# Edge sums of a graph layer: a plain addition with a source slot from a table, and index registers loaded in blocks

## What is computed

```
e     = edge_attr @ We                       # per edge
kj    = k[src] + e
alpha = sum(q[dst] * kj, per head) / sqrt(32)
ea    = exp(alpha - max over the edges of the same dst)
msg   = (v[src] + e) * ea
out   = segment_sum(msg, dst) / segment_sum(ea, dst) + x @ Ws + bs
```

## Time and profile before

| | |
|---|---|
| median of three runs | 2568.09 us |
| span of the profiled execution (the page gives no other time of it) | 2568.6 us |
| first and last rescale of the edge loop (start) | 284.0 and 1957.4 us |
| TensorE busy | 2382.9 us, 93% of the span |
| VectorE busy | 2037.0 us, 79% |
| GpSimd busy | 1811.8 us, 71% |
| ScalarE busy | 1577.5 us, 61% |

### The profile page before, as it was taken

The page is one execution under the profiler, slowest core; times in us unless marked ns, Lnnn a source line. Parts: engine busy times, 40 slices in busy tenths (PEclk is TensorE's granted clock), DMA queues, the critical chain, the costliest instruction groups (busy, mean ns, idle before and its releaser), DMA issues. The chain is left out here.

```text
span 2568.6 us, 67072 instructions
## 1 busy us (share of the span) xinstructions
PE 2382.9 (93%) x13310; PEld 1992.2 (78%) x13311; DVE 2037.0 (79%) x5261; ACT 1577.5 (61%) x4373; POOL 1811.8 (71%) x2136
## 2 busy tenths in 40 slices
PE   6998999999999999999999999999995657999998
PEld 2445788888888888888888888888883646999998
DVE  6865899999999999999999999999997773222222
ACT  1222677777777677777767777767774224666665
POOL 4123788888888888888888888888886104666666
PEclk9999999999999999999999999999998557999999
DMA  7326777777777777777777777777772753433443
GB/s 229 128 107 187 231 227 221 227 228 228 223 227 227 220 230 224 221 227 226 227 221 226 227 225 229 227 218 220 228 223 78 227 162 60 71 63 64 70 66 55
DMA packets 337693, 476.68 MB, mean 186 GB/s; under 512 B 61318, under 2 KB 268492, under 8 KB 337052
## 3 DMA queue, kind: packets, MB, share of 16 engines
q0 software_dynamic: 92576, 259.72, 37.8%
q1 hardware_dynamic: 238492, 213.23, 28.0%
q10 hardware_dynamic: 6288, 0.05, 0.1%
HBM read 425.40 MB, written 50.57 MB: 185 GB/s over the span
## 5 line engine op out<-in xcount | busy, mean ns | idle before, releaser
L809 POOL DMA_INDIRECT kv_ring<-vk_table,tab_c x880 | 860.6, 978 | 284.3 <-issue 208.2
L963 PE MATMUL ps_e<-we_sb,aT 128*128 128x256 f32 x3520 | 919.5, 384 | 27.9 <-DVE ve_ke L1050 21.6
L963 PEld LDWEIGHTS ps_e<-we_sb,aT 128*128 128x128 f32 x3520 | 601.0, 191 | 102.8 <-issue 48.6
L1044 DVE TENSOR_TENSOR ve_ke<-kv_ring,ps_e 128x512 f32<-128x512 f32 x880 | 599.9, 682 | 38.1 <-PE ps_e L967 24.0
L1014 PE MATMUL ps_u<-ve_ke,sel 128*128 128x264 f32 x1760 | 547.7, 393 | 20.3 <-DVE node_slots L1114 6.8
L819 POOL TENSOR_TENSOR ve_ke<-ve_ke 128x256 f32<-128x256 f32 x880 | 553.4, 633 | 18.5 <-ACT factor L936 4.9
L967 PE MATMUL ps_e<-q_slots,selT 128*128 x1760 | 517.6, 375 | 0.0
L896 ACT COPY aT<-ps_t 128x256 f32<-128x256 f32 x880 | 325.5, 370 | 310.1 <-PE ps_t L951 189.6
L1114 DVE SCALAR_TENSOR_TENSOR node_slots<-node_slots,same_tile,ps_u 128x264 f32 x880 | 423.0, 481 | 29.5 <-DVE node_slots L1099 10.6
L967 PEld LDWEIGHTS ps_e<-q_slots,selT 128*128 128x128 f32 x1760 | 335.1, 190 | 45.9
L1032 DVE TENSOR_REDUCE alpha<-ve_ke 128x8 f32<-128x256 f32 x880 | 365.3, 415 | 5.6 <-issue 3.6
(11 more groups left out here) (249 smaller groups left out, 2642.3 us busy)
## 6 DMA issues: line engine op xcount, KB each, us to landing
a_ring<-in_edge_attr SPq DMA_DIRECT2D x880, 128.0 KB
loc_c<-loc_table SPq DMA_DIRECT2D x220, 128.0 KB
kv_ring<-vk_table,tab_c POOLq DMA_INDIRECT x880
vk_table<-kv_out SPq DMA_DIRECT2D x49, 256.0 KB
skip_table<-skip_out SPq DMA_DIRECT2D x49, 128.0 KB
skip<-skip_table SPq DMA_DIRECT2D x7, 896.0 KB, 10.8
xn_table<-node_slots SPq DMA_DIRECT2D x7, 896.0 KB, 6.5
out<-node_slots SPq DMA_DIRECT2D x1, 6144.0 KB
```

The lines of the kernel that those rows point to most:

```text
L809: g.indirect_dma_start(out=kv_ring[:, i % N_KV, :], out_offset=None, in_=vk_table, in_offset=bass.IndirectOffsetOnAxis(ap=tab_c[:, c % N_T ...
L963: t.matmul(ps_e[i % 2][:, 0:D], aT[i % 2][:, k * P:(k + 1) * P], we_sb[:, k, :], start=(k == 0), stop=(k == KD - 1))
L1044: v.tensor_tensor(ve_ke[:, to:ke + 1:ke - to, 0:D], kv.rearrange("p (t d) -> p t d", t=2), e[:, None, :].to_broadcast([P, 2, D]), ALU.add) ...
```

## The change

- A second table `item_from` is made at the end of the first stage's table building: for an item it holds its own node tile if the item before has the same one, else the number NT + 2 = 51 of a new slot. That slot (264 columns behind the last) is cleared once by GpSimd.
- `add` becomes `to = source + ps_u` with both addresses from registers; the scalar column is gone from it.
- TensorE loads the 16 tile numbers of the next chunk in one instruction after `project` of step 13. VectorE loads 8 tile numbers and 8 source numbers by two instructions right after every eighth add, which is the add of step 4 and of step 12. The comparisons and assertions are gone.
- In the expert stage the four output tiles `y` lie in the space of `values`, no longer in tiles of their own.

```diff
-        node_slots = sb("node_slots", [P, NT + 2, SLOT])
+        sums_flat = sb("node_slots", [P, (NT + 2) * SLOT + UW])
+        node_slots = sums_flat[:, 0:(NT + 2) * SLOT].rearrange("p (j w) -> p j w", w=SLOT)
...
                 g.memset(node_slots[:, 0, 0:UW], 0.0).then_inc(first_cleared, 1)
+                g.memset(sums_flat[:, (NT + 2) * SLOT:(NT + 2) * SLOT + UW], 0.0).then_inc(first_cleared, 1)
...
                 then(v.tensor_tensor(same_tile[:, 1:IT], node_tile_rep[:, 1:IT], node_tile_rep[:, 0:IT - 1], ALU.is_equal))
+                then(v.scalar_tensor_tensor(out=from_rep[:, :], in0=node_tile_rep[:, :], scalar=float(NT + 2), in1=same_tile[:, :],
+                                            op0=ALU.subtract, op1=ALU.mult))
+                then(v.tensor_scalar(item_from, from_rep[64:65, :], float(NT + 2), None, ALU.add))
...
-                def node_tile_of(c, i):
-                    return pe.value_load(item_node_tile[0:1, bass.ds(c * CH + i, 1)], min_val=0, max_val=NT)
+                def node_tiles_of(c):
+                    return nc.values_load_multi_w_load_instructions(
+                        item_node_tile[0:1, c * CH:(c + 1) * CH], engines=[mybir.EngineType.PE], min_val=0, max_val=NT,
+                        skip_runtime_bounds_check_because="a count of at most NT steps")[1]
...
-                            project(c, i, n)
-                            if i + 1 < CH:
-                                n = node_tile_of(c, i + 1)
+                            project(c, i, tiles[i])
+                            if i == CH - 3 and c + 1 < NCH:
+                                next_tiles[:] = node_tiles_of(c + 1)
...
-                    meanwhile()
...
+                def slots_of(c, h):
+                    some = slice(c * CH + h * HALF, c * CH + (h + 1) * HALF)
+                    to, sofar = [nc.values_load_multi_w_load_instructions(
+                        row[0:1, some], engines=[mybir.EngineType.DVE], min_val=0, max_val=NT + 2,
+                        skip_runtime_bounds_check_because="a count of at most NT steps, or NT + 2")[1] for row in (item_node_tile, item_from)]
+                    return list(zip(to, sofar))
...
-                    v.scalar_tensor_tensor(out=to, in0=sofar, scalar=same_tile[:, m:m + 1], in1=ps_u[i % 2][:, 0:UW], op0=ALU.mult, op1=ALU.add
-                                           ).then_inc(s["acc_added"], 1)
+                    v.tensor_tensor(to, sofar, ps_u[i % 2][:, 0:UW], ALU.add).then_inc(s["acc_added"], 1)
...
+                            if i % HALF == HALF - 1 and m_of(c - back, i) + 1 < NCH * CH:
+                                ahead[:] = slots_of((m_of(c - back, i) + 1) // CH, (i // HALF + 1) % 2)
...
-            y = [sb7(f"y{i}", [P, D]) for i in range(4)]
+            y = [values[:, i, :] for i in range(4)]
```

More of the change, by code:

```diff
@@ L99, in gnn_ffn @@
         item_row = item_rows[32:33, :]
+        item_from = item_rows[64:65, :]
         chunk_tile = sb("chunk_tile", [P, NCH])
@@ L166, in gnn_ffn @@
             step_at = sb1("step_at", [NT, 1])
+            from_rep = sb1("from_rep", [P, IT])
             ii_i = sb1("ii_i", [P, IT], I32)
@@ L368, in _ @@
                         resets()
-                pool.wait_ge(first_cleared, 1)
+                pool.wait_ge(first_cleared, 2)
             @block.scalar
@@ L971, in emit @@
                 def emit(c, par, steps):
-                    n = node_tile_of(c, 0) if steps[0][0] == "score" else None
+                    if c == 0:
+                        next_tiles[:] = node_tiles_of(0)
+                    tiles = tuple(next_tiles)
                     for kind, i, back in steps:
@@ L1033, in reduce, with score @@
                                     ALU.add).then_inc(s["alpha_ready"], 1)
-                def score(c, par, i, meanwhile):
+                def score(c, par, i):
                     e = ps_e[i % 2][:, 0:D]
@@ L1102, in rescale, with m_of, add @@
                     dve.sem_inc(s["softmax_pace"], 1)
[L1104 to L1109, removed]
+                last_tile, ahead = [], []
+                HALF = CH // 2
+                def m_of(c, i):
+                    return c * CH + i
+                def slots_of(c, h):
[4 more added lines that the diff above has]
+                    return list(zip(to, sofar))
+                def add(c, i, n, source):
                     m = c * CH + i
-                    to, sofar = [sums_flat[:, bass.ds(k * SLOT, UW)] for k in (n, before)]
+                    to, sofar = [sums_flat[:, bass.ds(k * SLOT, UW)] for k in (n, source)]
                     dve.wait_ge(s["summed"], at("summed", m))
                     dve.wait_ge(s["acc_added"], at("acc_added", m - 1))
-                    v.scalar_tensor_tensor(out=to, in0=sofar, scalar=same_tile[:, m:m + 1], in1=ps_u[i % 2][:, 0:UW], op0=ALU.mult, op1=ALU.add
-                                           ).then_inc(s["acc_added"], 1)
+                    v.tensor_tensor(to, sofar, ps_u[i % 2][:, 0:UW], ALU.add).then_inc(s["acc_added"], 1)
                 def emit(c, par, steps):
[L1119 to L1126, removed]
                     for kind, i, back in steps:
                         if kind == "score":
-                            score(c, par, i, lambda: load_next(i))
+                            score(c, par, i)
                         elif kind != "add":
@@ L1133, in emit @@
                         else:
[L1134 to L1137, removed]
+                            if i % HALF == 0 and not ahead:
+                                ahead[:] = slots_of(c - back, i // HALF)
+                            n, source = ahead.pop(0)
                             if i == 0:
-                                rescale(c - back, before)
-                            add(c - back, i, n, before)
+                                rescale(c - back, last_tile[0] if last_tile else n)
+                            add(c - back, i, n, source)
                             last_tile[:] = [n]
+                            if i % HALF == HALF - 1 and m_of(c - back, i) + 1 < NCH * CH:
+                                ahead[:] = slots_of((m_of(c - back, i) + 1) // CH, (i // HALF + 1) % 2)
                 over_chunks(dve, emit, what="add", parts={3: "scan", 4: "scan_back", 6: "own", 7: "least", 8: "shift"})
@@ L1616, in put @@
                         out=out, out_offset=bass.IndirectOffsetOnAxis(ap=put_i[:, b:b + 1], axis=0),
-                        in_=y[b % 4][:, :], in_offset=None, bounds_check=N - 1, oob_is_err=False,
+                        in_=y[b % 4], in_offset=None, bounds_check=N - 1, oob_is_err=False,
                         compute_op=ALU.add).then_inc(y_stored[b % 4], 16)
```

4 lines of the change are left out of this document (2 added, 2 removed).

## The result

The changed kernel took 2620.02 us (median of four runs, 2618.46 to 2621.64) against 2567.34 of the kernel before (2561.28 to 2568.68): ratio 1.0214, 95% interval 1.0202 to 1.0227. It is 2.1% slower, where 2558 us was forecast.

The account below looks back on a forecast made before the run. TensorE and VectorE were taken to share the edge loop, the lead passing about once a chunk each way. Gains 0.31 + 0.10 - 0.20 = 0.21 us a chunk, 11.6 us; 2568.6 - 11.6 + 1.8 = 2558.8, forecast 2558 us, range 2548 to 2568.

Parts of the forecast that it names:

- The loads added: VectorE's two block loads between an add and the next score: stall 0.20 us a chunk at step 12, none at 4.
- the lower end: Price of a load of eight numbers on VectorE: 304 ns, like a single load; the upper end was 2.43 us.
- the second rival: VectorE's block loads: each further number costs a register operation, up to 0.085 us; 2584 to 2685 us; chance 0.25, partly shared.
- the wait and the handing over: VectorE's sequencer before the score at step 12: 0.05 us for the wait, about 0.2 to hand the score over.
- Nearest in kind: Reason for pricing a block load at 304 ns: like the trace's single load, one instruction, eight numbers 32 bytes side by side.
- the other eleven are covered by TensorE: Only VectorE's adds of steps 4, 5, 6, 7, 13 gain, 0.31 us a chunk; the other eleven gain nothing.
- The addition: VectorE's plain add takes 419 ns instead of 481, 62 less; five adds count, 0.31 us a chunk.
- The loads taken away: Without single loads behind VectorE's scores, reduces at steps 4 and 13 come 0.05 us earlier each: 0.10 us a chunk.
- The lead: Edge loop: VectorE sets the pace in steps 4 to 8 and 13 to 14, TensorE elsewhere; VectorE edits count only there.
- TensorE's block: TensorE's block load replaces a single load and its two checks, 301 ns for the load alone, hidden: costs nothing.
- The first stage: Two 880-column operations join a VectorE chain TensorE waits for: 1.8 us late, bounds 0 and 2.
- The signs named in advance: Profile after: block loads 0.3 us; forecast wrong if the score idles at step 4 or rescales come closer than 30.5 us.

Follow-up runs that it names:

- the table of sizes: Kernel before with VectorE register loads of 1 to 16 numbers from several table places ahead of the edge loop; four such kernels: 2568.71, 2589.94, 2603.13, 2611.61 us.
- the stall runs: Kernel before with loads of 4, 8 or 16 numbers after two adds: steps 5 and 13 2619.53 (4), 2716.15 (8); steps 1 and 10 2575.11, 2657.25, 2875.91 us.
- the table above: Idle and hidden time of block-load kernels against pairs: changed kernel 2620.02 us; its loads merged into one of 16 2564.97, moved to steps 15 and 9 2652.16, doubled 2817.18.
- the pairs: Kernel before with the plain addition and table, VectorE loading tile and source of one item as two numbers inside each score: 2543.29 us, ratio 0.9913.
- the run with the loads moved: Changed kernel with VectorE's two block loads moved from the adds of steps 4 and 12 to those of 15 and 9: 2652.16 us, ratio 1.0339.

## Why the prediction was wrong

**The failed step is "The loads added".** It took the lower end, 0.304 us for a load of eight; the load took 0.812. That is inside the second rival's range (0.44 to 0.90), near its upper end, so the rival's price came true, and through it alone the time lies inside the stated range; its mechanism did not. Each further number cost 0.073 us ((0.812 - 0.304) / 7) and not a register operation's 0.019, and elsewhere loads go by fours (the table of sizes). The working itself holds: with 0.812 it gives 2 x 0.812 + 0.25 - 0.67 = 1.20 us at step 12 and 2 x 0.812 + 0.31 - 1.00 = 0.93 at step 4, against 1.11 and 0.78 measured. Most of the difference is the wait and the handing over, taken as 0.25, where 0.145 passed from the end of the loads to the score. (One number of the forecast's own range is off: 0.2 at step 4 is 55 x 0.2 = 11 us, not 8.) "Nearest in kind" chose the end on one argument, that eight numbers are one instruction and 32 bytes; an instruction can still do its work number by number, as the stall runs show with 0.22 us each. There the Trainium skill's "Runtime: NRT & Kernel Launch", section "Instruction fetch mechanics" (some 200 ns a register, even in bulk; it speaks of loads from HBM), fits these loads from SBUF too; from a multiple of four it does not, 0.25 us for four. The floor of about 600 ns in the Trainium skill's "DMA: Bandwidth & Descriptors", section "Latency and other measured facts", is contradicted for them by 0.31 for one number.

**The second rival's sum was too high.** At 0.81 it would say 2568.6 + 55 x (0.93 + 1.20 - 0.41) + 1.8 = 2665 us; the span is 2618. The shorter idle time (1.89 for 2.13) is 13 us of that, the first stage 1.8. Some 32 us, 0.58 us a chunk, are left. They fit the step "the other eleven are covered by TensorE": that holds while TensorE is the bound. With stalls on VectorE its own length counts, and so would the eleven adds, 11 x 0.062 = 0.68 us; the table above shows 0.3 to 0.5 hidden. No run takes these adds apart.

**The addition: right.** 420 ns against 419. Where no stall hides it, the gain is that of the prediction: 0.31 + 0.10 us a chunk, 22.6 us; the pairs gained 22.5 (2565.8 to 2543.3). The agreement is closer than the runs can tell (their interval is some 4 us either way), and that it is five adds and no others was not tried.

**The loads taken away: right.** The reduce stands 0.60 behind the score everywhere, and the kernel that keeps the old addition and takes the loads out of the score gained 8.3 us where 0.10 a chunk makes 5.5.

**The lead: right in the kernel before, misapplied later.** Stalls placed in VectorE's stretches cost 98% of their length, elsewhere all but 0.3 to 0.8 us a chunk. The run with the loads moved missed its range because its stalls of 2.4 us a chunk were far above that slack.

**TensorE's block: right,** at 1.10 us a load and no cost. **The first stage:** its length was right (1.32 us late where 1.8 was the estimate), but none of it reached the loop; the lower bound, 0, was the true one.

The signs named in advance told it: the load's own row (0.81) decided at once, the score idled at step 4, and the rescales were 32.0 us apart.

## What to carry to other kernels

A register load is work of the engine's sequencer, so ask first what stands behind it: inside a long instruction (0.68 us here) 880 loads of two numbers left the next instruction on time, between two instructions 220 loads of eight made the kernel 77 us slower than that. If the trace shows no load of the size in question, both ends of its price belong in the forecast, and one run with loads of several sizes and places settles it. A gain on an engine that is not the bound is slack that a new stall may eat: weigh the two together.

## What was not expected of the hardware

- A load's time goes by fours and by place: 0.25 us for four numbers from a multiple of four, 0.22 for each single one elsewhere, so that eight numbers take 0.60 or 1.85 us (and 0.81 in the changed kernel, which stays open).
- The rescale, whose operands both lie in SBUF, has a median of 418 ns in the changed kernel and of 594 in the earlier trace rows. In both traces it takes about 418 where GpSimd's own two-tensor operation isn't running and mostly about 594 where the two overlap by 0.3 us (a few overlapped ones took 419 to 473); no run took that apart.
